# First attention: two pieces of values in one run, projections and output products in other units

## The reference

```python
q, k, v, kp = (_heads(x @ W.T, B, T) for W in (W_Q, W_K, W_V, W_K_prime))
out_std = softmax(q @ k.T / SCALE) @ v          # per head
out_p   = softmax(q @ kp.T / SCALE) @ v
out = alpha * out_std + (1.0 - alpha) * out_p   # heads side by side
return out @ W_O.T                              # added to h
```

## Time and profile before

| | |
|---|---|
| profiled execution | 1851.4 us, its span 1849.6 us |
| median of three runs | 1849.86 us |
| TensorE (matmuls) busy | 1758.3 us, 95% of the span |
| VectorE, ScalarE, GpSimd busy | 1005.2, 678.9, 408.1 us |
| the first attention's eight turns | from 137 to 709 us of the span |
| TensorE's granted clock, mean | 0.982 of full |

### The profile page before, as it was taken

The page is one execution under the profiler, slowest core; times in us unless marked ns, Lnnn a source line. Parts: engine busy times, 40 slices in busy tenths (PEclk is TensorE's granted clock), DMA queues, the critical chain, the costliest instruction groups (busy, mean ns, idle before and its releaser), DMA issues. The chain is left out here.

```text
span 1849.6 us, 29111 instructions
## 1 busy us (share of the span) xinstructions
PE 1758.3 (95%) x9935; PEld 1119.1 (61%) x9935; DVE 1005.2 (54%) x2073; ACT 678.9 (37%) x1290; POOL 408.1 (22%) x415
## 2 busy tenths in 40 slices
PE   7989999999999997899999999998999999999997
PEld 3324444344444433677766656656666668999997
DVE  6597877768778866788874555442211111222121
ACT  2106656556566675454532333223111110111110
POOL 2101021120211001789841112210121211000100
PEclk9989999999999998999999999999999999999999
DMA  6733532525425111000046000000010003332311
GB/s 188 133 65 66 91 79 40 95 53 89 78 40 102 17 48 39 34 0 0 0 189 207 1 0 0 0 1 1 23 37 17 34 20 106 134 140 102 106 31 33
DMA packets 111955, 112.84 MB, mean 61 GB/s; under 512 B 11455, under 2 KB 104433, under 8 KB 111858
## 3 DMA queue, kind: packets, MB, share of 16 engines
q1 hardware_dynamic: 98610, 83.21, 19.9%
q10 hardware_dynamic: 9600, 18.92, 2.8%
q0 software_dynamic: 3648, 9.46, 1.4%
HBM read 78.51 MB, written 32.93 MB: 60 GB/s over the span
## 5 line engine op out<-in xcount | busy, mean ns | idle before, releaser
L927 DVE TENSOR_REDUCE mx<-ps_a 128x1 f32<-128x384 f32 x768 | 380.2, 550 | 54.8 <-PE ps_a L567 53.0
L791 ACT ACTIVATE prob<-ps_a 128x768 f32<-128x768 f32 (+1 forms) x512 | 306.2, 650 | 108.9 <-PE ps_a L580 107.4
L567 PE MATMUL ps_a<-w,qs 96*128 96x384 bf16 x768 | 244.0, 337 | 10.3 <-DVE mx L927 5.5
L580 PE MATMUL ps_a<-qs,w 100*128 100x384 bf16 x768 | 209.2, 332 | 6.1 <-issue 3.4
L2134 PEld LDWEIGHTS ps_e<-xTr,w 128*128 128x128 f32 x1792 | 204.4, 192 | 2.2 <-issue 0.8
L2134 PE MATMUL ps_e<-xTr,w 128*128 128x128 f32 x1792 | 204.7, 275 | 0.6 <-DVE xTr L2307 0.6
L567 PEld LDWEIGHTS ps_a<-w,qs 96*128 96x128 bf16 x768 | 74.6, 98 | 188.4 <-DVE mx L927 103.1
L591 PE MATMUL ps_a<-prob,vp 128*32 128x384 f32 x1536 | 164.0, 500 | 0.0
L2071 PE MATMUL ps_e<-xT_all,w 128*128 x448 | 145.7, 486 | 0.0
L2197 ACT ACTIVATE gel_r<-ps_e 128x512 f32<-128x512 f32 x56 | 33.4, 597 | 280.3 <-PE ps_e L2134 280.3
L1593 PE MATMUL ps_m<-w 128*128 128x352 f32 x384 | 126.0, 473 | 9.8 <-ACT w L1767 5.3
(11 more groups left out here) (265 smaller groups left out, 2536.1 us busy)
## 6 DMA issues: line engine op xcount, KB each, us to landing
w<-parts_dram SPq DMA_DIRECT2D x192, 96.0 KB, 5.1
w<-in_L_ffn_W_dram ACTq DMA_DIRECT2D x18, 1024.0 KB, 8.2
parts_dram<-w SPq DMA_DIRECT2D x24, 576.0 KB, 3.4
qs<-parts_dram SPq DMA_DIRECT2D x96, 96.0 KB, 3.9
prob<-in_x_dram SPq DMA_DIRECT2D x24, 256.0 KB
w<-in_L_ffn_W_dram SPq DMA_DIRECT2D x6, 1024.0 KB, 12.9
grouped_x<-empty_row SPq DMA_DIRECT2D x1, 4352.0 KB, 24.3
grouped_h<-empty_row SPq DMA_DIRECT2D x1, 4240.5 KB, 32.7
```

Source lines behind the costliest of these rows:

```text
L567: mm = pe.matmul(ps[:, r % 3, 0:T], qs[0:NS, b, u // 2, t * P:(t + 1) * P], ks[0:NS, b, u % 2, u // 2], start=True, stop=True)
L580: mm = pe.matmul(ps[:, 4 + t, 0:T], ks[0:NS + 4, b, kp, hh, t * P:(t + 1) * P], qs[0:NS + 4, b, hh], start=True, stop=True)
L791: act.activation(prob[:, g % 2, j, ts.start:ts.stop], ps[:, 4 + ts.start:4 + ts.stop, 0:T], ACT.Exp).then_inc(exp_done.sem, 1)
L927: dve.tensor_reduce(at, ps[:, r % 3, 0:T], AX.X, ALU.max).then_inc(ring_free.sem, 1)
```

## The change

Of the three pieces of values of a group, the first two are issued one behind the other in unit j = 1, the third in unit j = 2, and unit j = 3 has none. The table of steps in bank 3 is filled in another way: the projection of values goes from units 3 and 5 to 2 and 3, five of the six other projections from 13, 14, 15, 17, 18 to 14, 15, 18, 19, 22, the output products from 19 and 21 to 23 and 26. All engines read the same table, so ScalarE's, VectorE's and GpSimd's parts move along. No instruction is added or taken away.

```diff
@@ BANK3
-    BANK3 = {0: ("turn_outputs", 6), 3: ("values", 0), 4: ("turn_outputs", 7), 5: ("values", 1),
+    BANK3 = {0: ("turn_outputs", 6), 2: ("values", 0), 3: ("values", 1), 4: ("turn_outputs", 7),
              6: ("turn_y", 0), 7: ("turn_y", 1), 8: ("turn_outputs", 0), 9: ("inputs", 0), 10: ("inputs", 1),
-             11: ("project", 0), 12: ("turn_outputs", 1), 13: ("project", 1), 14: ("project", 2),
-             15: ("project", 3), 16: ("turn_outputs", 2), 17: ("project", 4), 18: ("project", 5),
-             19: ("output", 0), 20: ("turn_outputs", 3), 21: ("output", 1), 24: ("turn_outputs", 4),
+             11: ("project", 0), 12: ("turn_outputs", 1), 14: ("project", 1), 15: ("project", 2),
+             16: ("turn_outputs", 2), 18: ("project", 3), 19: ("project", 4), 20: ("turn_outputs", 3),
+             22: ("project", 5), 23: ("output", 0), 24: ("turn_outputs", 4), 26: ("output", 1),
              28: ("turn_outputs", 5)}
+    PIECES = {1: (0, 1), 2: (2,)}
@@ turn of the tensor engine
-                        if j and g:
-                            values(i, b, g - 1, j - 1)
-                        elif j and prev:
-                            values(i - 1, 1 - b, GROUPS - 1, j - 1)
+                        for t in PIECES.get(j, ()):
+                            if g:
+                                values(i, b, g - 1, t)
+                            elif prev:
+                                values(i - 1, 1 - b, GROUPS - 1, t)
```

## The result

The changed kernel takes 1869.43 us (median of four runs, 1866.35 to 1870.4), the kernel before 1849.26 in the same series (1846.35 to 1853.23): 1.0094 times the time, 95% interval 1.0076 to 1.0113, or 20.2 us more. The profiled execution takes 1869.53 us, its span 1867.8.

A forecast was written before the change was run, and what follows sets the result against it. TensorE sets the pace (busy 72.4 of 75.57 us per image), VectorE having little air. Terms 2.5 + 11.5 + 1.9 - 1 = +14.9 on the profiled 1851.4 give 1866.3, so 1865 for the median; 8-in-10 range 1842 to 1880.

The forecast's parts named there:

- a doubled run saves: Merging two pieces of values saves TensorE 0.235 us per run, 1.88 per full image, 14.8 over 63 groups.
- units 7 and 8: Turns of y: two copies to SBUF join ScalarE's exponentials, 3.27 us against a content of 2.71; +0.50 per full image.
- unit 15: Transposition waits for VectorE's maxima after unit 14's projection, so the unit stays 4.20 us without its piece; +0.88.
- wait in units 19, 20, 23: Bank 3 steps with no values between them wait for VectorE's low part, about 0.45 us each.
- units 27 and 28: Ring matmuls wait for maxima behind the moments of output 1 in unit 26; +1.14 us per full image.
- light pair: Fourth unit without a step plus the next first unit: 2.85 to 2.87 us against a content of 2.38; cost 0.47.
- unit 31: Transposition waits on the last maximum with no piece between ring matmuls: 2.42 us, +0.42 per full image.
- image 0; images 1 to 5; image 6: Summed losses by image: +2.5 us in the first, +11.5 in the five full ones, +1.9 in the seventh.
- the eighth image, to the weights: Image without a ring, paced by ScalarE: taken as -1 us, bounds -2.5 and +2.5.
- The clock: Rival: waits of units 27 and 28 lower TensorE's clock in six images, 2.3 us each, total 1880; chance 0.10.
- The DMA chain: Stacks written from the last projection, now in unit 22: hidden in full images, 0 to 1 us shown in the first; taken as 0.
- The last turn: Eighth image: doubled pieces uncovered, +0.65 us in some six groups, but VectorE's hole for output 1 gone; taken as -1.

The follow-up runs named there:

- Experiment 1: The kernel before with the doubled run alone (two pieces in unit 1, one in unit 2, none in 3), old table of bank 3: 1865.70 us.
- experiment 8: The kernel before with inputs normalized behind unit 5, and doubled runs only in units 1 to 3 (images 1 to 6) and 9 to 11 (images 0 to 5): 1844.58 us.
- experiment 4: The changed kernel with all three pieces in one run in unit 1, none in units 2 and 3: 1867.93 us.
- experiment 2: The kernel before with new places for bank 3's projections and output products, but one piece in each of units 1 to 3: 1855.23 us.
- 5: The changed kernel with VectorE's moments taken of 16 of 256 channels in all images except the last two; output differs: 1864.74 us.
- experiment 6: The changed kernel with VectorE normalizing the inputs of image i + 2 behind unit 5 instead of at the head of the turn: 1872.34 us.
- 3: The changed kernel with one piece in each of units 29 to 31, as before the change: 1863.32 us.
- 7: The kernel before with VectorE normalizing the inputs of image i + 2 behind unit 5: 1845.81 us.

## Why the prediction was right

It said 1865 us and 14.9 more; it is 1869.4 and 20.2 more, within its range, but a quarter of the loss was not in the sum. By its steps, in a full image:

| step | predicted, us | measured, us |
|---|---|---|
| a doubled run saves | 0.235 | 0.24 (unit 5: 2.52 instead of 1.875 + 0.885) |
| units 7 and 8 | 3.27 | 1.45 + 1.85 = 3.30 |
| unit 15 | 4.20 | 4.20 |
| wait in units 19, 20, 23 | 0.45 each | 0.45, 0.40, 0.45 |
| units 27 and 28 | 4.06 | 3.93 (images 5 and 6: 3.68) |
| light pair (27 and 28 of image 0) | 2.85 to 2.87 | 1.39 + 1.47 = 2.86 |
| unit 31 | 2.42 | 2.38 to 2.57 (without the loop's pause) |
| units 0 and 1 | as before + 0.65 = 5.19 | 5.95 |
| units 2 to 31, images 1 to 5 | +1.65 each | +1.39 to 1.74 |
| image 0; images 1 to 5; image 6 | +2.5; +11.5; +1.9 | +2.0; +16.2; +3.0 |
| the eighth image, to the weights | -1 | +0.1 |

The mechanism was right: what is taken from TensorE is less than what it was hiding, and it is lost in the units that have no values. Experiment 1 shows that against the view that TensorE's work decides, and experiment 8 by its opposite; experiment 4 agrees in its total, but in full images most of TensorE's saving was kept. Two pieces in one run left TensorE waiting for VectorE and ScalarE, which read its banks (+0.45 at bank 3, 1.4 us as the least unit). The Trainium skill's rule on the emptying of PSUM (TensorEngine Tiling (Array Packing), section PSUM Bottleneck), that tiling speeds up TensorE and not the emptying, fits in kind only: both kernels pack four column tiles, and the banks waited for are not the one of the pieces.

Two terms were too small. *The clock* was a rival of its own, put at units 27 and 28 and at 2 to 3 us an image, with a chance of 0.10; it did come true, but at the seam. The prediction named as a sign of being wrong that the clock leaves 1.00 inside an image; it did so, in units 0 and 1 of all of images 1 to 6 (before the change of image 3 alone), and in this point the prediction was wrong. It costs 0.8 us in image 4 and 1.6 in image 6. The row that could have told it is 1.08 us of wait for the maxima behind a unit 31 without values, then 0.35 more: in the kernel before 0.65 and 0.38 stood there with the clock at 1.00. Units 0 and 1 take 4.8 us more than walked in images 2 to 6 together, most of what is missing, and 2.1 more in image 1. *The DMA chain* in the first image: "0 to 1 us shown" was a wait of 1.63. The walk had found 19.0 us of room against some 19 needed; 20.9 were needed (20.8 in experiment 2), and the row it read, stacks still moving from 350 to 352, allows anything from 18.7 to 20.7. The last turn was put 1 us too low; there TensorE's wait for VectorE's add (2.06 us) moved from unit 20 to 24 and did not go, and VectorE's hole shrank only from 2.80 to 1.83. The terms for image 0 (+2.5 against +2.0) and for units 27 and 28 were too large, so the total is a little nearer than its parts. One reading was off without effect: VectorE comes back to the maxima 2.52 us after the projection in the earlier trace rows, not 2.49.

## What to carry to other kernels

A saving on the busiest engine is worth what the unit has to do next without waiting: before removing work, write down for each unit which chain of the other engines is nearly as long, and what the removed instructions were covering. Here a sum of busy times (95% on TensorE) promised -15 us, and a walk over 32 units with three chains +15; measured were +20. If two short units come together, ask whether the first waits of the next stage become long enough to lower the clock.

## What the runs showed of the hardware

- Two and three pieces in column tiles run on without a gap: 8, 16 and 24 records take 0.85, 1.50 and 2.14 us; entering and leaving costs 0.24 us together.
- The seam of two images has a wait of 1.06 to 1.08 us for the maxima and 0.2 to 0.5 more where unit 31 has no values, of 0.65 and as much more where it has. The clean seams are those ahead of images 2, 4, 5 and 6; ahead of image 1 there can be the DMA wait, and ahead of image 3 is the loop's pause of over 3 us. In the five kernels with the long wait (the changed one, experiments 1, 4, 5 and 6) the clock is at its lower level behind 14 of 20 clean seams; in the five with the short one (the kernel before, 2, 3, 7, 8) behind none of 20. With all seams it is 22 of 30 and 7 of 30: all ten behind the loop's pause, and five of the ten ahead of image 1.
- Waits of 0.25 and 0.61 us in units 27 and 28 did not lower it. At the lower level two score matmuls take 0.84 us instead of 0.49. That the gate goes by how busy the engine has lately been is also what the Trainium skill says (TensorE: Matmul & The Clock Gate, What's actually happening); these rows agree in direction.
- What stays open: why the clock falls behind 14 of the 20 clean long waits and not behind all. The seam ahead of image 6 has the same instructions in the changed kernel and in experiment 6; it falls in the one (units 0 and 1: 6.12 us) and not in the other (4.50).
